# Scores of a 32-wide-head self-attention as 64-row products on quarters of the TensorE array

## What is computed

```python
q = heads(Wq, bq); k = heads(Wk, bk); v = heads(Wv, bv)      # (32, 16, 64, 32)
scores = jnp.einsum('bhqd,bhkd->bhqk', q, k) / SCALE
causal_mask = jnp.arange(seq)[None, :] > jnp.arange(seq)[:, None]
scores = jnp.where(causal_mask, jnp.float32(-1000000000000.0), scores)
probs = jax.nn.softmax(scores, axis=-1)
attn = jnp.einsum('bhqk,bhkd->bhqd', probs, v)
return attn @ Wm + bm
```

## Time and profile before

| | us |
|---|---|
| median of 3 runs (range) | 1332.13 (1331.94 to 1332.32) |
| the profiled execution | 1331.58 |
| its span | 1329.8 |
| TensorE busy | 1303.1 (98%) |
| VectorE busy | 731.4 (55%) |
| ScalarE busy | 343.8 (26%) |
| score products (L2061), busy | 31.2 in 256 records |

### The profile page before, as it was taken

How to read it: one execution, slowest core, us unless ns; L and a number is a source line. 1 busy time by engine, 2 the same in 40 slices (tenths; PEclk the granted TensorE clock), 3 DMA queues, 4 the chain that set the end, 5 groups by cost and what they waited for, 6 DMA issues and landing times.

```text
span 1329.8 us, 20744 instructions
## 1 busy us (share of the span) xinstructions
PE 1303.1 (98%) x7187; PEld 811.8 (61%) x7188; DVE 731.4 (55%) x1370; ACT 343.8 (26%) x614; POOL 169.8 (13%) x173
## 2 busy tenths in 40 slices
PE   6999999999999999999999999999999999999998
PEld 3443444444444444457888888899996677777743
DVE  4445455544444444468877777666434444544446
ACT  2211111111111111134444444442212333322200
POOL 0000000000000000003000005503423200000054
PEclk9999999999999999999999999999999999999999
DMA  9999999999999999812576752142669889999997
GB/s 336 411 393 391 394 388 391 390 394 394 390 388 389 386 388 387 315 55 99 180 251 253 267 204 88 50 159 80 260 220 320 277 280 300 305 295 297 297 341 244
DMA packets 122194, 387.28 MB, mean 291 GB/s; under 512 B 12160, under 2 KB 34688, under 8 KB 122016
## 3 DMA queue, kind: packets, MB, share of 16 engines
q1 hardware_dynamic: 117024, 369.87, 76.0%
q0 software_dynamic: 5120, 16.78, 3.5%
HBM read 328.41 MB, written 58.20 MB: 291 GB/s over the span
## 4 chain that ended last, share of the span: by engine, by line
PE 92%; DMA 4%; SPq 1%; DVE 1%; issue 1%; ACT 0%; ACTq 0%; DVEq 0%
PE ps L1953 14%; PE ps L1856 13%; PE ps L2025 11%; PE ps L2015 10%; PE ps L2303 5%; PE ps L1905 4%; PE ps L1916 4%; PE ps L1908 4%; PE ps L1812 3%; PE ps L2401 2%; PE ps L2393 2%; PE ps L2061 2%; PE ps L1931 2%; PE ps L2319 2%; PE ps L2322 2%; PE ps L2325 2%
## 5 line engine op out<-in xcount | busy, mean ns | idle before, releaser
L784 ACT ACTIVATE arena<-ps 128x512 f32<-128x512 f32 (+2 forms) x164 | 77.7, 495 | 556.6 <-PE ps L1916 180.3
L1953 PE MATMUL ps<-arena 128*64 128x512 f32 (+1 forms) x832 | 192.3, 594 | 0.0
L1856 PE MATMUL ps<-arena 128*64 128x512 f32 (+1 forms) x1024 | 178.7, 505 | 2.7 <-DMA arena<-ctx_t 1.9
L2025 PE MATMUL ps<-split 128*128 128x256 f32 x1344 | 170.6, 285 | 1.1 <-DVE split L1324 1.1
L2025 PEld LDWEIGHTS ps<-split 128*128 128x128 f32 x1344 | 163.6, 191 | 7.1 <-issue 6.3
L2015 PE MATMUL ps<-split 128*128 128x512 f32 x648 | 157.7, 396 | 0.3 <-DVE arena L1390 0.3
L1856 PEld LDWEIGHTS ps<-arena 128*64 128x64 f32 x1024 | 67.5, 138 | 121.4 <-issue 118.0
L2015 PEld LDWEIGHTS ps<-split 128*128 128x128 f32 x648 | 119.2, 188 | 28.6 <-issue 3.5
L1226 DVE SCALAR_TENSOR_TENSOR arena<-arena,hbar 128x512 f32<-128x512 f32 x128 | 90.5, 749 | 70.4 <-PE ps L1916 69.0
L1953 PEld LDWEIGHTS ps<-arena 128*64 128x64 f32 (+1 forms) x832 | 58.3, 137 | 112.4 <-issue 111.7
L1159 DVE TENSOR_REDUCE small<-ps 128x1 f32<-128x1601 f32 x15 | 27.4, 1826 | 118.8 <-PE ps L1856 118.8
(11 more groups left out here) (223 smaller groups left out, 1818.4 us busy)
## 6 DMA issues: line engine op xcount, KB each, us to landing
arena<-ctx_n SPq DMA_DIRECT2D x128, 768.0 KB, 16.4
arena<-ctx_t SPq DMA_DIRECT2D x122, 800.5 KB, 20.0
split<-parts_low SPq DMA_DIRECT2D x39, 768.0 KB, 7.2
split<-parts_low SPq DMA_DIRECT2D x39, 512.0 KB, 4.9
moe_in<-zero SPq DMA_DIRECT2D x3, 3328.0 KB, 13.4
moe_out<-arena SPq DMA_DIRECT2D x39, 256.0 KB, 4.9
stage_raw<-w1t SPq DMA_DIRECT2D x8, 768.0 KB, 5.4
parts_high<-split SPq DMA_DIRECT2D x8, 768.0 KB, 7.1
```

What stands on the lines that cost most here:

```text
L784: return nc.scalar.activation(o, i, ACT.Copy)
L1856: last = mm(bank(n)[S * h:S * (h + 1), 0:w], qT[:, k, S * h:S * (h + 1)], ctxT[h][:, k, at_j:at_j + w], start=(k == 0), stop=(k == KD - 1))
L1953: last = mm(bank(7)[S * h:S * (h + 1), :], ET[0:w, c, S * h:S * (h + 1)], ctxN[h][0:w, c, :], start=(c == 0), stop=(c == JC - 1))
L2025: last = mm(dst[:, 2 * P * m:2 * P * (m + 1)], w[a][:, k, c], tokens[b][:, k, :], start=(k + i == 0), stop=(k == KD - 1 and i == 2))
```

## The change

A key block is cut in two along the rows of the array. Of the four heads of a group, heads 0 and 1 (partitions 0 to 63, `u = 0`) and heads 2 and 3 (partitions 64 to 127, `u = 1`) get a product each: 64 rows, 64 stationary columns, 128 moving columns, in place of one with 128 rows and 256 columns. A tile has 16 such products where it had 8. Each stands on one quarter of the array: its row half is given by `u`, its column half by the batch `b`. The row halves write different banks: bank 4 for `u = 0`, bank 5 for `u = 1`.

`Kbd` has 128 columns per group and batch in place of 256, so each of its two buffers is 1024 elements per partition in place of 2048, and GpSimd zeroes half as much. The buffers that lie behind it (`Vbd`, `sm`, `prob`, `PT`, `attn`) move down. The copies by ScalarE are as many and as large as before. The order of the heads in the two banks is now all groups' heads 0 and 1, then all groups' heads 2 and 3; mask, softmax and transposes work on it as it is, and `attend_b` picks the pair of heads by `pair_at(g)`, so that the rest keeps the natural order. `scores` has one more instruction on TensorE's stream, an increment of a semaphore that nobody waits for (`hold`, until now `pool_go` and used by GpSimd alone), between the wait for the key copies and the first product.

```diff
@@ -34,6 +34,7 @@
 NP = 5
 H, HD = 16, 32
 HG = P // HD
+HR = HG // 2
 VW = 2 * HD + 2
 FS = 1024
 KF = FS // P
@@ -194,8 +195,8 @@
         assert used[0] == SPLIT, used[0]
         qhT = carve(KD, 2 * P)
         khT = carve(KD, 2 * P)
-        Kbd = [carve(KD, 2, HG * S) for _ in range(2)]
-        assert used[0] - 2 * KD * HG * S <= 2 * KD * J + 2 * JC * D, used[0]
+        Kbd = [carve(KD, 2, HR * S) for _ in range(2)]
+        assert used[0] - 2 * KD * HR * S <= 2 * KD * J + 2 * JC * D, used[0]
         Vbd = [carve(2, H // 2, VW) for _ in range(2)]
         sm = carve(H, S)
         prob = carve(H, S)
@@ -309,6 +310,10 @@
             return (ctxT[h][:, 1:KD, JM * P:J],
                     bank(4 + g % 4)[:, 0:(KD - 1) * JT].rearrange("p (k n) -> p k n", n=JT))
 
+        def pair_at(g):
+
+            return H // 4 * (g % HR) + g // HR
+
         def h1T_bank(i, first):
 
             return bank(4 if first and i == 0 else 0 if first else i)
@@ -341,7 +346,7 @@
         CONSTS, KBD0, VBD0, KBD1, VBD1, ZERO, IOTA = 9, 10, 13, 14, 17, 18, 21
         raw_in, high_done, low_done, parts_out = (
             [sem(f"raw_in{i}") for i in range(2)], sem("high_done"), sem("low_done"), sem("parts_out"))
-        pool_go = sem("pool_go")
+        hold = sem("hold")
         first_done, first_act, first_dve, first_scores = (
             sem(n) for n in ("first_done", "first_act", "first_dve", "first_scores"))
         dve_step = sem("dve_step")
@@ -885,7 +890,8 @@
                     act.wait_ge(s_done, t - 1)
                 for h in range(HG):
                     r = slice(HD * h, HD * (h + 1))
-                    copy(Kbd[i][r, :, :, S * h:S * (h + 1)],
+                    e = h % HR
+                    copy(Kbd[i][r, :, :, S * e:S * (e + 1)],
                          khT[r, :, P * i:P * (i + 1)].rearrange("p m (b j) -> p m b j", b=2)).then_inc(kbd_ready, 1)
 
             def pt_copy(t, first):
@@ -2041,7 +2047,8 @@
                 pe.wait_ge(vbd_ready, 4 * (t + 1))
                 for g in range(H // 2):
                     for b in range(2):
-                        ma = mm(bank(6 + g // 4)[S * b:S * (b + 1), VW * (g % 4):VW * (g % 4 + 1)], PT[:, g, S * b:S * (b + 1)],
+                        ma = mm(bank(6 + g // 4)[S * b:S * (b + 1), VW * (g % 4):VW * (g % 4 + 1)],
+                                PT[:, pair_at(g), S * b:S * (b + 1)],
                                 Vbd[i][:, b, g, :], start=True, stop=True)
                 ma.then_inc(av_done, 1)
@@ -2056,10 +2063,14 @@
 
             def scores(t, i):
                 pe.wait_ge(kbd_ready, HG * (t + 1))
+                pe.sem_inc(hold, 1)
                 for m in range(KD):
-                    for b in range(2):
-                        ms = mm(bank(4 + m // 2)[S * b:S * (b + 1), HG * S * (m % 2):HG * S * (m % 2 + 1)],
-                                qhT[:, m, P * i + S * b:P * i + S * (b + 1)], Kbd[i][:, m, b, :], start=True, stop=True)
+                    for u in range(2):
+                        r = slice(HR * HD * u, HR * HD * (u + 1))
+                        for b in range(2):
+                            ms = mm(bank(4 + u)[S * b:S * (b + 1), HR * S * m:HR * S * (m + 1)],
+                                    qhT[r, m, P * i + S * b:P * i + S * (b + 1)], Kbd[i][r, m, b, :],
+                                    start=True, stop=True)
                 ms.then_inc(s_done, 1)
 
             def project_v(i):
```

More of the change, by code:

```diff
@@ L682, in add_b_qv @@
                 pool.wait_ge(hc_ready, t + 1)
-                pool.sem_inc(pool_go, 1)
+                pool.sem_inc(hold, 1)
                 if first:
```

## The result

| | before | after |
|---|---|---|
| median of 4 runs (range), us | 1332.22 (1331.94 to 1333.68) | 1319.74 (1315.23 to 1321.82) |
| the profiled execution, us | 1331.58 | 1321.82 |
| its span, us | 1329.8 | 1320.1 |

The ratio is 0.990, with an interval of 0.9873 to 0.9926: the change makes the kernel faster by 12.5 us by the medians, against 10.5 forecast. The interval, times the time before, is 1315.3 to 1322.4 us; the forecast of 1321.6 lies in it, near its edge. A second set of runs gave 1320.57 (5 runs) against 1332.16 (22 runs of the kernel before), 11.6 us.

What follows compares the result with a forecast made beforehand. TensorE, 98% busy, was taken as the bound. 14 calls at 0.78 us gave 10.9, less 0.4 at the end: 10.5 us, so 1332.1 - 10.5 = 1321.6 us, range 1319 to 1332.5.

Steps and rivals of the forecast that it cites:

- The mechanism: Self-attention score calls on TensorE: four quarters work at once, shortening 14 steady calls, 10.9 us gained; main case 70%.
- The rival that row halves take turns: Score calls: the two row halves don't overlap, a call stays at 1.9 us, the kernel at 1332.4; chance 12%.
- the one of a drain at each change of half: Score calls: each change of row half drains the array, a call takes 2.6 us, 10 us slower, 1342; chance 8%.
- The Trainium skill's rule for a weight load: Score calls: 64 columns load in 53 ns whatever the rows; 32 loads in line take 1.7 us, no gain.
- What the Trainium skill says on packing: Score calls: products on different row strips run together and row and column packing compose; cited against the turns rival.
- The price of a call: Steady score call on TensorE: 1.10 us in place of 1.88, a gain of 0.78 us in each of 14 calls.
- bounds of 1.01 and 1.14: Score call length: 1.01 us if the array limits, 1.14 at the record rate of `attend_b`; forecasts 1320.4 and 1322.1.
- the zeroing: GpSimd's zeroing of a key buffer, 1.81 us, is halved; its readers' products stand behind `values`, so 0 gained.
- waits longer by 0.8 us at the first two tiles: First two tiles: calls end in waits on `values` and `h1_low`, so shorter calls lengthen the waits and gain nothing.
- The end: Behind the last score call: TensorE's transposes wait 0.44 us for a VectorE chain, about 0.4 us lost.
- The slack ahead of the first projection: Steady pair: `h1_low` still ends 0.47 us before TensorE needs it, so no wait.
- The signal: Increment of `hold` on TensorE ahead of the scores: taken as 0; 2.4 us given back if it emptied the array.

Runs made afterwards that it cites:

- the values in quarters: Changed kernel with the products with the values also cut into 64-row, 33-column products per head, 32 a tile in place of 16: 1320.52 us, ratio 0.9904.
- The room run: Changed kernel with the key buffers in their old room and with their old zeroing, quarter products kept: 1321.49 us, ratio 0.9927.
- the first profile: Profiled execution of the changed kernel in its first set of four runs, the slowest of them: 1321.82 us.
- The repeat: Changed kernel measured and profiled once more with no edit: 1320.57 us, ratio 0.9909.

## Why the prediction was right or wrong

**The mechanism was right.** TensorE was the bound, the quarters stream at once, and the call's length is the whole of it in the steady part: made short without quarters the gain is there, made long with quarters it is gone. The rival that row halves take turns, and the one of a drain at each change of half, are out: the call is 1.034 us. The Trainium skill's rule for a weight load (TensorE: Matmul & The Clock Gate, section LDWEIGHTS), taken as 32 loads one behind the other, gave 1.7 us; they take 0.86 us busy in a call. So the loads of different quarters don't queue. The rule's 53 ns for one load of 64 columns is not contradicted: with the values in quarters, groups of four loads start 55 to 58 ns apart. What the Trainium skill says on packing (the same page, section "Packing small matmuls"), that products on different row and column strips run together, the trace bears out: the call is 1.034 us.

**The price of a call was too high by 0.07 us: the step that failed.** I had bounds of 1.01 and 1.14 and took 1.10, "nearer to the measured rate" of `attend_b`. It is 1.034. The array limit was the right end, and the reason against it was wrong: that weight loads, at 28 ns each, were just level with the array. The rate of `attend_b` was one record on each column half every 58 ns, of which its 66 columns fill 54.5. It is not a rate of loads: quarters pass four loads in these 58 ns and not two, as the experiment with the values shows. 14 calls x 0.844 is 11.8 us, not 10.9: 0.9 us.

**The second step that failed: the zeroing was priced at nothing; with the smaller room it was worth 0.7 us.** I had costed it by who waits for it (the key copies, which are early) and not by who runs beside it. VectorE's subtraction at the second tile, 1.2 us elsewhere and 2.2 there, was visible in the trace of before, with GpSimd at work beside it. The room run shows that the old zeroing and room bring it back. This gain is luck: it hangs on how far GpSimd's instruction has come when the subtraction starts, and the same meeting at 805.21 goes the other way in the first profile. Of the forecast of waits longer by 0.8 us at the first two tiles, the first came true (0.30 to 1.15 us); the second did not (1.13 as before), and with the old zeroing and room it does come (2.04).

**The end**: a wait of 0.39 us at the place named; the delay is 0.6 us against 0.44 taken. The slack ahead of the first projection was 0.50 against 0.47 forecast. **The signal** costs nothing, as taken.

**Not forecast:** the 0.7 us wait before 813.71 in the first profile, where a subtraction stretched to 2.29 us stands beside GpSimd's splitting of weights. The repeat doesn't have the loss; the old-room run and the one with the values in quarters have it (the last pair takes 31.79 and 31.84 us, with subtractions of 2.08 and 2.16). I had looked for slack in an ordinary pair only.

The sum over the self-attention: 11.8 (calls) + 0.7 (second tile) - 0.6 (end) - 0.4 (steps into and out of a pair's calls, 0.05 us a pair, not traced further) = 11.5 us, as the repeat measures, and 10.6 in the first profile, whose last pair is 0.9 longer. The forecast of 10.5 came near to this because its errors cancel in part: it had the calls 0.9 and the second tile 0.7 too low, the end 0.2 and the steps 0.4 too high. What the medians show beyond 11.5 (12.5 in the first set) I put down to the rest of the kernel, whose spread is larger than that, above all in the expert stage; no run ties it to the change. **The range** had its lower end at 1319, 1.4 us below what the call's own bound gave; with runs of one kernel that differ by 6 us it should have gone some 3 us lower. Where it reached down was wrong, not where it reached up.

## What to carry to other kernels

Small products that use half the rows and half the columns of the array run four at a time if neighbours in the stream take turns in both halves; order them so, since the same products grouped by row half shortened a call by 0.36 us in place of 0.84. The row halves wrote different banks in every run here; one bank for both was not tried. Cut by the columns streamed, and, with weights of 64 columns, stop where a group of records streams in less than 58 ns: from 66 to 33 columns only 0.02 us a call was left to gain. And before an operation on another engine is costed at nothing, look for who runs beside it, not only for who waits for it.

## What the runs showed of the hardware

- Four quarters of the array stream at once: 16 products of 64x64 weights and 128 columns in float32 (32 records) in 0.835 us from first to last start, 109 ns for each group of four where the columns take 106.
- TensorE starts work for an idle row half past records that wait for the busy one: with all of half 0 first in the stream, half 1 began at 0.50 us with six of its matmul records still ahead; with four products of half 0 first, at 27 ns, again with six ahead.
- Records in one quarter, with their weight loads of 64 columns, followed each other at 58 ns at the least, where 33 columns stream in 27. Within a group, starts are 7 ns apart.
- VectorE's subtraction over 128x1024 elements takes 1.2 us in a steady pair. Where it starts while an instruction of GpSimd is under way, it ends 1.08 us after that instruction: 1.3 to 2.3 us in 19 of 20 cases. Where GpSimd's instruction starts after the subtraction, it is GpSimd's that is longer: at the last tile of each profile, 0.03 to 0.04 us behind it, 2.3 us in place of 1.3, and the subtraction takes its 1.22. This is read from where the rows stand; no run took GpSimd's work away.
